# A four-layer graph network on one core: the attention layer's result kept by edge in DRAM and gathered, instead of scatter-added to the node table

## The reference, cut to what matters

```
n = lambda x: relu(layernorm(x))                      # before every layer
# 1 GCN
x = x + segment_sum(edge_weight * (n(x) @ W0)[dst], src) + b0
# 2 GAT, 4 heads of 32 columns
y = leaky(n(x), 0.01) @ W1.T + b1;  g = y @ Wg.T
alpha = leaky(sum(g * att_src)[src] + sum(g * att_dst)[dst], 0.2)
coeff = softmax of alpha over the edges with one dst
x = x + leaky(segment_sum(g[src] * coeff, dst) + bias_g, 0.01) @ W2.T + b2
# 3 hypergraph: d_e counts the edges of a hyperedge, d_v sums hw by node, both at least 1
z = n(x) / sqrt(d_v);  he = min(dst, M - 1)
f = segment_sum(z[src], he) * hw / d_e
x = x + (segment_sum(f[he], src) / sqrt(d_v)) @ W.T + b
# 4 tensor product: w = silu(edge_attr_8 @ Wfc1) @ Wfc2 weights products of edge_attr_4 with
#   the linearly mapped features of src, 256 values by edge
x = x + b_n * (segment_sum(features(n(x)[src] @ B1, edge_attr_4, w), dst) @ B2)
return x
```

## The kernel before, in words

| stage | from about (us) | POOL issues |
|---|---|---|
| 1 sort of the edges, table filled | 0 | 196 gathers of edge records |
| 2 GCN | 509 | 196 gathers by dst_s, then 196 adds |
| 3 GAT: projections, logits | 1126.6 | 392 gathers (src_d and dst_d) |
| 4 softmax over runs | about 1640 | none |
| 5 GATSUM: weighted sums, W2 | 1697 | 196 adds |
| 6 HYP: sums by hyperedge | 2080.9 | 196 gathers by src_d |
| 7 HYPSUM: sums by src, L2, edge weights of TP | 2344 | 196 gathers and 196 adds in turn |
| 8 TP | 2972.4 | 196 gathers by src_d, then 196 adds |

## Time and profile before

### The profile page before, as it was taken

How to read it: one execution, slowest core, us unless ns; L and a number is a source line. 1 busy time by engine, 2 the same in 40 slices (tenths; PEclk the granted TensorE clock), 3 DMA queues, 4 the chain that set the end, 5 groups by cost and what they waited for, 6 DMA issues and landing times.

```text
span 3591.9 us, 33806 instructions
## 1 busy us (share of the span) xinstructions
PE 1832.7 (51%) x7735; PEld 1375.6 (38%) x7735; DVE 1493.1 (42%) x4375; ACT 969.3 (27%) x2608; POOL 2675.4 (74%) x2284
## 2 busy tenths in 40 slices
PE   0000017777201899994999623376666656775000
PEld 0000005555101777773776423343433335665000
DVE  6874315555101444445333257722222216997000
ACT  0000014444101455551111135532222224554000
POOL 0767777778887777770888877778888887778887
PEclk9999997767555555555555555555555557998555
DMA  2999813345443222220555456655555555667443
GB/s 85 286 294 333 285 38 86 86 74 68 37 36 44 53 54 54 54 54 22 75 73 72 48 120 156 156 117 103 103 103 103 104 93 155 177 172 119 37 36 34
DMA packets 380201, 377.04 MB, mean 105 GB/s; under 512 B 76369, under 2 KB 307635, under 8 KB 379823
## 3 DMA queue, kind: packets, MB, share of 16 engines
q0 software_dynamic: 156800, 133.81, 28.1%
q1 hardware_dynamic: 182834, 209.37, 18.4%
q10 hardware_dynamic: 40512, 33.32, 3.8%
HBM read 227.20 MB, written 149.12 MB: 105 GB/s over the span
## 4 chain that ended last, share of the span: by engine, by line
POOL 36%; issue 10%; PE 4%; DMA 2%; DVE 1%; ACT 0%; ACTq 0%; POOLq 0%; DVEq 0%; SPq 0%
POOL out_dram L581 21%; POOL work L567 10%; POOL big L567 5%; PE bank L849 1%; PE bank L848 1%; DMA out_dram<-work,idx_add_d 1%; PE bank L745 1%; DMA out_dram<-big,idx_add_d 0%; ACT work L1069 0%; DVE work L1679 0%; DVE work L1414 0%; DMA work<-out_dram,idx_src_d 0%; DVE work L1571 0%; PE bank L904 0%; DVE work L1419 0%
## 5 line engine op out<-in xcount | busy, mean ns | idle before, releaser
L1571 DVE TENSOR_TENSOR_SCAN work<-work,bank 128x512 f32<-128x512 f32 (+1 forms) x343 | 426.5, 1265 | 396.1 <-PE bank L745 227.5
L567 POOL DMA_INDIRECT work<-out_dram,idx_src_d x392 | 374.8, 956 | 124.1 <-issue 118.9
L581 POOL DMA_INDIRECT out_dram<-work,idx_add_d x196 | 308.5, 1574 | 152.2 <-ACT work L1147 93.3
L1069 ACT ACTIVATE work<-work 128x128 f32<-128x128 f32 x784 | 317.4, 481 | 322.3 <-DVE work L1566 223.6
L581 POOL DMA_INDIRECT out_dram<-work,idx_add_s x196 | 312.6, 1595 | 60.6 <-issue 59.1
L745 PE MATMUL bank<-ident,work 128*128 128x128 f32 x588 | 160.7, 429 | 382.4 <-ACT work L1069 199.8
L581 POOL DMA_INDIRECT out_dram<-big,idx_add_s x196 | 305.7, 1560 | 62.2 <-issue 54.0
L581 POOL DMA_INDIRECT out_dram<-big,idx_add_d x196 | 304.6, 1554 | 62.1 <-issue 55.2
L567 POOL DMA_INDIRECT work<-rec_d,idx_e_s x196 | 216.3, 1103 | 80.5 <-issue 58.5
L745 PEld LDWEIGHTS bank<-ident,work 128*128 128x128 f32 x588 | 113.1, 221 | 424.9 <-issue 154.4
L567 POOL DMA_INDIRECT work<-he,idx_last_s x196 | 192.9, 984 | 75.5 <-issue 59.4
(11 more groups left out here) (284 smaller groups left out, 4411.3 us busy)
## 6 DMA issues: line engine op xcount, KB each, us to landing
out_dram<-big SPq DMA_DIRECT2D x71, 726.0 KB, 8.2
big<-in_x_dram SPq DMA_DIRECT2D x71, 704.0 KB, 7.0
work<-flags_src SPq DMA_DIRECT2D x98, 256.0 KB, 3.8
work<-flags_dst SPq DMA_DIRECT2D x98, 256.0 KB, 3.5
edge_w<-big SPq DMA_DIRECT2D x49, 512.0 KB, 3.3
work<-edge_w ACTq DMA_DIRECT2D x49, 512.0 KB
work<-flags_clip SPq DMA_DIRECT2D x49, 256.0 KB, 4.4
he<-work SPq DMA_DIRECT2D x49, 256.0 KB, 2.5
```

The costliest lines, as they stand in the source:

```text
L567: g_.indirect_dma_start(to, None, table_ap, bass.IndirectOffsetOnAxis(ap=f[:, at_:at_ + 1], axis=0)).then_inc(of_rows(name).of(G), 16)
L581: g_.indirect_dma_start(table[:, :], bass.IndirectOffsetOnAxis(ap=of[:, at_:at_ + 1], axis=0), row, None, compute_op=ALU.add).then_inc(add ...
L1069: last = S_.activation(h[:, t * P:(t + 1) * P], v(t), ACT.Relu, bias=stat[:, 8 + t:9 + t], scale=stat[:, t:t + 1])
L1571: return V.tensor_tensor_scan(to, flag_r[G.place][rows, :], of, before if G.from_(1) else 0.0, ALU.mult, ALU.add)
```

## The change

The attention layer's result is no longer added to `table`.

- **Stage 5** stores it by edge in DRAM (`d1`, one row by position in dst order, only the last of a run being the sum); row EP of `d1` is zero. The projected rows are stored to DRAM in stage 3 (`gat_h`) and loaded by SP in stage 5, since `big` now holds the source rows of stage 3. The constant is subtracted on DVE (`cols[:, 2:3]` in `leaky`) instead of by the one-row matmul.
- **Stage 3** gathers the source rows into `big`, where they stay for stages 6 and 8, and the target rows into a ring of four.
- **Stage 6** gathers from `d1` by `run_d`: for each edge, the position that holds the sum of the run whose target is this edge's source, or EP if there is none. It adds that to `big`, in place.
- **Stage 7** also stores its own result by position in src order (`s2`); it is still added to `table`.
- **Stage 8** gathers from `s2` by `sum_s` into a ring of four, adds it and a constant to `big`'s row, reads `d1` by position, and DVE's new `keep` makes (TP result × scalar + `d1` row), so that one add to `table` carries both layers. ACT's `keep` is gone.
- **The two indices** are made on the chip at the end of stage 2 (`MAPS`): PE and DVE rank every source key among the sorted dst keys, in 49 groups (`steps`, `rank`, `counts`), and then turn both results from src order into dst order by one-hot matmuls, in 49 groups (`onehots`, `place`). Two more column transposes and a backward spread are added at the end of stage 1.

The diff, cut to its core:

```diff
@@ POOL
+            def body(G):                      # stage 3
+                if G.from_(UNROLL):
+                    pool.wait_ge(GAT["taken"], G.g - (UNROLL - 1))
+                for of, to in ((idx["src_d"], big[...]), (idx["dst_d"], rows_r[G.place])):
...
-            every_group(adds("GATSUM", idx["add_d"], GATSUM["kept"], dl4_r))
-            added.wait_all(pool, "GATSUM")
             stage_end(pool, 5)
-            every_group(gathers("HYP", table, [idx["src_d"]], HYP["taken"]))
+            every_group(gathers("HYP", d1_dram, [idx["run_d"]], HYP["taken"], D, in_r))
...
-            every_group(gathers("TP", table, [idx["src_d"]]))
-            rows_in.wait_all(pool, "TP")
+            every_group(gathers("TP", s2_dram, [idx["sum_s"]], TP["taken"], D, in_r))
             every_group(adds("TP", idx["add_d"], TP["kept"]))
@@ SP, stage 5
+                load_flags(sp, G, "dst", GATSUM)
+                sp.wait_ge(GATSUM["h"], G.g - (UNROLL - 1))
+                sp.dma_start(in_r[G.place], at(h_dram, G, 512)).then_inc(h_in.of(G), 16)
+                store(G.before(UNROLL))       # waits GATSUM["kept"], stores 256 KB to d1
@@ PE, end of stage 2
+            def rank(G):
+                for t in range(GROUP):
+                    T.matmul(o, step_e[G.slot][:, c], jump_e, start=True, stop=False)
+                    last = T.matmul(o, step_o[G.slot][:, c], jump_o, start=False, stop=True)
+            def place(G):
+                for t in range(GROUP):
+                    last = T.matmul(bank[4][:, 0:2 * TILES], hot_r[G.slot][:, t * P:(t + 1) * P],
+                                    place_r[G.slot][:, t * 2 * TILES:(t + 1) * 2 * TILES], ...)
@@ PE, stage 5
-                    T.matmul(o, one[0:1, :], negc1[0:1, :], start=True, stop=False)
-                    last = T.matmul(o, z_r[G.slot][:, ...], wts["W2T"][:, :], start=False, stop=True)
+                    last = T.matmul(bank[4 + G.slot][:, ...], z_r[G.slot][:, ...], wts["W2T"][:, :], start=True, stop=True)
@@ DVE, end of stage 2
+            def steps(G):
+                keys_at.wait(dve, "MAPS", G)
+                done(V.tensor_scalar(step_e[G.slot], flag_r[G.place][0:LANES, :], dl[:, 0:1], None, ALU.is_ge))
+                V.tensor_scalar(step_o[G.slot], flag_r[G.place][0:LANES, :], dl[:, P:P + 1], None, ALU.is_ge)
+            def counts(G):
+                dve.wait_ge(MAPS["ranked"], G.g + 1)
+                for t in range(GROUP):
+                    for k, (c, op) in enumerate(((le, ALU.is_le), (eq, ALU.is_equal))):
+                        done(V.tensor_scalar(junk[2 * t + k], w, key[:, t:t + 1], None, op, ALU.add, accum_out=c[:, t:t + 1]))
...
+            def onehots(G):
+                for t in range(GROUP):
+                    done(V.tensor_scalar(hot_r[G.slot][:, ...], iota_f[:, 0:P], row[:, t:t + 1], None, ALU.is_equal))
+                    for k in range(2):
+                        ins = V.tensor_scalar(place_r[G.slot][:, o:o + TILES], iota_f[:, 0:TILES], col[:, t:t + 1],
+                                              of[k][:, t:t + 1], ALU.is_equal, ALU.mult)
@@ DVE, stage 3: one 1024-wide subtract becomes three of 512
-                done(V.tensor_tensor(t4(v8[G.slot]), r[:, :, 0:D], over(wts["K1"][:, :], W8), ALU.subtract))
+                done(V.tensor_tensor(t4(v8[G.slot])[:, 0:GROUP], rs[:, :, 0:D], over(wts["K1"][:, :], GROUP), ALU.subtract))
+                done(V.tensor_tensor(rs[:, :, 0:D], rs[:, :, 0:D], over(wts["K2"][:, :], GROUP), ALU.subtract))
+                done(V.tensor_tensor(t4(v8[G.slot])[:, GROUP:W8], rd[:, :, 0:D], over(wts["K1"][:, :], GROUP), ALU.subtract))
@@ DVE, stage 5
-                V.scalar_tensor_tensor(z_r[G.slot], t1_r[G.slot], 0.01, t1_r[G.slot], ALU.mult, ALU.max)
+                done(V.scalar_tensor_tensor(z_r[G.slot], t1_r[G.slot], 0.01, t1_r[G.slot], ALU.mult, ALU.max))
+                need(order.off)
+                V.tensor_scalar(z_r[G.slot], z_r[G.slot], cols[:, 2:3], None, ALU.subtract).then_inc(GATSUM["z"], 1)
@@ DVE, stage 8
+                V.tensor_tensor(t4(x3_r[G.slot]), t4(in_r[G.place]), over(wts["K2"][:, :], GROUP), ALU.add
+                                ).then_inc(TP["taken"], 1)
+                dve.wait_ge(TP["taken"], G.g + 1)
+                done(V.tensor_tensor(t4(x3_r[G.slot]), t4(x3_r[G.slot]), r[:, :, 0:D], ALU.add))
...
+            def keep(G):
+                dve.wait_ge(TP["delta"], G.g + 1)
+                d1_in.wait(dve, "TP", G)
+                for t in range(GROUP):
+                    ins = V.scalar_tensor_tensor(to[:, t * ROW:t * ROW + D], bank[7][:, c], b4[:, 4 * t + 1:4 * t + 2],
+                                                 d1_r[G.slot][:, c], ALU.mult, ALU.add)
```

More of the change, by code:

```diff
@@ L1144, in keep @@
                 act.wait_ge(GATSUM["delta"], G.g + 1)
[L1145 to L1148 removed]
+                if G.from_(2):
+                    d1_stored.wait(act, "GATSUM", G.before(2))
+                S_.copy(dl_r[G.slot][:, 0:512], bank[4 + G.slot][:, :]).then_inc(GATSUM["kept"], 1)
             def body(G):
@@ new lines, in body @@
+            def body(G):
+                steps(G)
+                if G.from_(1):
+                    counts(G.before())
+            for_groups(dve, body, order)
+            counts(group(NG - 1))
+            dve.wait_ge(MAPS["counted"], NG)
+            need(order.off)
+            link(V.tensor_scalar(run_f, n_blk, float(P), float(-P - 1 - EP), ALU.mult, ALU.add))
+            link(V.tensor_tensor(run_f, run_f, n_le, ALU.add))
+            link(V.tensor_tensor(n_eq, n_eq, n_blk, ALU.min))
@@ L1818, in body @@
                     chain2(G.before(2))
+                if G.from_(3):
+                    keep(G.before(3))
             for_groups(dve, body, order)
```

234 lines of the change are left out of this document (179 added, 55 removed).

## The result

The changed kernel takes a median of 3783.3 us (3775.2 to 3786.7, 4 runs) against 3597.2 us (3595.1 to 3600.5, 4 runs) for the kernel before: ratio 1.051, 95% interval 1.049 to 1.053. It is slower, as forecast, but by 186 us where 101 were forecast; 3783 lies inside the range of 3625 to 3825, 83 us above the predicted 3700. The profiled execution took 3784.3 us, its span is 3782.5.

What follows compares the result with a forecast made beforehand. POOL was taken to bound stage 5 and stage 8's adds, with DVE and PE idle 197 us in stage 2. Terms -205 + 151 + 149 + 3 + 4 = +102 on 3593.7 gave 3696, predicted median 3700 us, range 3625 to 3825.

Steps and rivals of the forecast that it cites:

- Stage 2, +151 forecast: End of stage 2: index work of 349 us on DVE and PE outlasts POOL's cover of 197 us, +151 us.
- its upper bound: Stage 2's counting loop: at most 4.8 us a group, against 3.9 taken.
- The rival of the cold placing loop: Stage 2's placing loop: TensorE stays at 1.2 GHz, +127 us, 3827 us in all; chance 0.17.
- Stage 5, -205: Stage 5: POOL's adds go, DVE sets 3.3 us a group, 179 us against 384, -205 us.
- The rival of a round over SP: Stage 5: SP's store and loads set 5 us a group, -122 instead of -205, 3783 us; chance 0.08.
- Stages 3 and 4: Stage 3: the last store of `gat_h` must land before the barrier, +3 us.
- Stage 8, +149 forecast: Stage 8: gathers follow DVE at 8.85 us a group, so POOL's adds start later, +149 us.
- Stage 6, +4 forecast: Stage 6: DVE's iteration is near POOL's 5.0 us and in-place addressing may cost a little, +4 us (0 to +10).

Runs made afterwards that it cites:

- experiment 7: Changed kernel with 1024 zero rows, its eight counting instructions a group writing no accumulated count: counting iteration 3.00 us instead of 3.10 (whole time 4177.6 us).
- Experiment 3: Changed kernel with stage 8's gathers and adds issued in turn on POOL: 3634.9 us, ratio 1.010 to the kernel before.
- Experiments 1: Changed kernel with 1024 zero rows behind d1 instead of one: 3713.7 us, ratio 1.032 to the kernel before; stage 6 263.9 us.
- experiment 2: Kernel before, with all gathers of stage 6 reading the table's one zero row: 3724.8 us, ratio 1.036; stage 6 387.8 us.

## Why the prediction was right, and where it was not

The path that each term names is the one that the trace shows, but for one: stage 6. The 88 us that the forecast's sum is short of are +64 in stage 6, +17 in stage 8, +8 in stages 3 and 4, +4 in stage 5, +1 in stage 7 and -6 up to stage 3. That 3783 us lies in the range is in part luck: the range was made wide for the index loops, stage 5 and DVE's iteration in stage 8, with at most 10 us for stage 6, where 68 came.

- **Stage 2, +151 forecast, +145 measured: right in mechanism, and near in size partly by luck.** Three errors largely cancel. DVE starts the index work 9 us later than I took (its last instruction of the layer is the reciprocal at 936.4 instead of 927.6). The counting loop lasts 159 us (940.3 to 1099.6) instead of 191, the placing loop 165 (1102.1 to 1267.6) instead of 147: +9 - 32 + 18. An iteration of the counting loop takes 3.10 us where I had 3.9, less than even my lower bound of 3.3:

```profile
1002.70 0.47 DVE L1739 TENSOR_SCALAR work<-work 98x512 f32<-98x512 f32 x1
1003.09 0.48 DVE L1740 TENSOR_SCALAR work<-work 98x512 f32<-98x512 f32 x1
1003.48 0.34 DVE L1750 TENSOR_SCALAR_CACHE_REDUCE work<-bank,key_src 128x128 f32<-128x128 f32 x1
1003.75 0.08 DVE L1750 DVE_READ_ACCUMULATOR work<-bank,key_src  x1
1003.75 0.34 DVE L1750 TENSOR_SCALAR_CACHE_REDUCE work<-bank,key_src 128x128 f32<-128x128 f32 x1
...
1005.79 0.49 DVE L1739 TENSOR_SCALAR work<-work 98x512 f32<-98x512 f32 x1
```

The trace shows the two instructions of which the Trainium skill speaks ("VectorE: DVE Perf Modes", section "Two Vector instructions with no wait between them"). But the read of 0.08 starts with the next comparison, and experiment 7 prices it at 0.01 each, where I took 0.075; so the loop is not near its upper bound, as I had it by that rule. The comparison itself was priced at 0.26 and takes that. The placing loop takes 3.3 to 3.4 us a group instead of 3.0.
- **The rival of the cold placing loop: refuted.** PE ran it at a granted clock of 0.97 to 1.00 from 1110 us on, 2.4 GHz, 89% busy:

```profile
1150.00:1200.00 50.00, 44.60 (x124) 22.23 (x125) 48.15 (x184) 0.00 (x0) 0.00 (x0) 1.00 0.00 0
```

- **Stage 5, -205: right.** From the first load of `gat_h` at 1853.3 to stage 6 are 182.8 us, against 383.9: -201. Its iteration is 3.3 to 3.5 us (1902.10, 1905.61, 1908.90):

```profile
1902.10 0.69 DVE L1866 TENSOR_TENSOR work<-work,al 128x512 f32<-128x512 f32 x1 [0.46 <-DMA work<-gat_h]
1902.71 0.69 DVE L1874 SCALAR_TENSOR_TENSOR work<-work 128x512 f32<-128x512 f32 x1
1903.43 0.48 DVE L1876 TENSOR_SCALAR work<-work,cols 128x512 f32<-128x512 f32 x1
1903.84 1.27 DVE L1668 TENSOR_TENSOR_SCAN work<-work,bank 128x512 f32<-128x512 f32 x1
1905.61 0.69 DVE L1866 TENSOR_TENSOR work<-work,al 128x512 f32<-128x512 f32 x1 [0.51 <-DMA work<-gat_h]
```

The rival of a round over SP was there in small: DVE waits about 0.5 us in these groups for `gat_h`, 19.8 us in the stage, where that rival needed 1.7 a group and a pace of 5 us. Its price was 3783 us, the very time that was measured, but the path is another.
- **Stages 3 and 4**, +3 forecast, came to +11: stage 3's gathers last 499 us from the first to the last (1271.7 to 1770.6), 9 more than before (1126.6 to 1616.7), and what lies between them and stage 5 another 2.
- **Stage 8, +149 forecast, +166 measured: right in mechanism, the iteration a little too small.** DVE takes 9.02 to 9.52 us (3200.06, 3209.08, 3218.60) instead of 8.85:

```profile
3207.23 1.10 DVE L1998 SCALAR_TENSOR_TENSOR big<-bank,sc_d,work 128x128 f32 x4
3208.25 0.68 DVE L1963 TENSOR_TENSOR work<-work,w_K 128x512 f32<-128x512 f32 x1
3209.08 0.69 DVE L1966 TENSOR_TENSOR work<-work,big 128x512 f32<-128x512 f32 x1 [0.15 <-DVE work L1963]
```

The additions came as priced: 1.10 for `keep` in L1998, 0.68 and 0.69 for the two tensor_tensors; 0.83 lie from the first to the second where I had 0.72, and in one group of four DVE stands another 0.37 before the first. ACT's turn of 0.36 inside the group is no part of the difference; it stood there before too:

```profile
3102.45 0.18 DVE L1565 RECIPROCAL work<-work 128x4 f32<-128x4 f32 x1 [0.36 <-ACT work L1062]
```

POOL waits for DVE, as forecast (us in total, times, longest): 160 us in 40 groups, 4.0 each where I had 3.8.

```profile
POOL work L640 <- DVE work L1963: 160.0, 40, 4.6
```

The last gather thus comes late and the first add 411 us after the first gather, where I had 396. Experiment 3 shows that the forecast named the right cause, the adds behind the tied gathers.
- **Stage 6, +4 forecast, +68 measured: the step that failed.** The prediction said that "about 80% of the gathers read the one zero row", and put this at nothing since stage 7's gathers read one row in 55% of the cases "and take no longer for it". That compares shares, and the price can't be seen on POOL, which takes 0.94 us for a gather with the one row or without it. It is in the DMA engines: 138 ns a row. Experiments 1 and 2 show that it is the one row (its share is 80%, next to nothing and 100% there); that stage 7 escapes by its slower pace is the reading under experiment 2, which no run tested. From the first gathers on the engines are full, and what shares them is late: DVE waited 75.8 us for flags and ACT 49.7 for the stores of `he` (us in total, times, longest), and neither wait stands in stage 6 of the kernel before.

```profile
DVE work L1668 <- DMA work<-flags_clip: 75.8, 21, 6.7
POOL work L640 <- DVE big L1907: 62.3, 24, 6.1
...
ACT work L1277 <- DMA he<-work: 49.7, 19, 6.1
```

POOL, which had set the pace before, waits 62.3 us for DVE in turn. With this term at +68 the forecast's sum would have been +166, 3764 us.

## What to carry to other kernels

An index that says "none" by pointing at one row of zeros can be a hot spot: spread it over some rows (1024 gave back 70 us; sixteen did as much for the engines' time), and look for its price in the share of the DMA engines, not in the time of the gathers on POOL. When a change takes an operation off an engine and puts a dependence on another, look at what stands behind the newly tied instructions in program order: here 196 adds stood behind 196 gathers that had only just become slow, and issuing them in turn gave back 148 of 166 us. A sum of separate errors can come out near: add up what each term measured before calling the working right. And an idle stretch of one engine is worth only the distance to the next bound: POOL's 141 us gave 42, since TensorE was 90% busy already.

## What the runs showed of the hardware that was not expected

- Reads of one DRAM row of 512 or 528 bytes by indirect DMA came 14 to 15 ns apart at best. A gathered row cost the DMA engines 138 ns on average when 80% of the reads went to the one row and 190 when all did, instead of 30 to 46. Transfers that share the engines landed later: 8.8 us for a 256 KB store against 2.5, 10.5 for a 256 KB load against 4.4.
- The chips of these runs differ by 7.7% for the kernel before. On three of the four, engines other than POOL nearly stop while POOL issues gathers back to back (DVE busy 3.2 of 50 us against 49.0 on the first), and not while it issues adds. The instructions that do start have their usual length (a 128-column matmul of L851 0.35 us against 0.37), but TensorE starts a matmul only every 2.8 us. POOL's own issue is the same on both kinds, 1.25 us from gather to gather. What stops the others was not settled. These chips took 276 us more for the kernel before, and 400 for the changed one.
